# The split of the next expert weights is put before the copies of the combine weights on ScalarE and VectorE

## The reference

```python
scores = softmax(x @ gate_w.T)                  # 16 experts
topk_w, topk_ids = top_k(scores, 6)
combine = einsum('tk,tke->te', topk_w, one_hot(topk_ids, 16))
for e in range(16):                             # inner width 176
    out += combine[:, e, None] * (silu(x @ g_e.T) * (x @ u_e.T)) @ w2_e.T
out += (silu(x @ sg.T) * (x @ su.T)) @ sw2.T    # shared expert, inner width 352
```

## Time and profile before

| what | value |
|---|---|
| median of 3 launches | 911.11 us (910.43 to 911.59) |
| the profiled launch, its own time | 910.82 us |
| its span in the trace | 909.0 us |
| PE busy | 887.6 us (98%) |
| DVE, ACT, POOL busy | 615.3 us, 424.0 us, 101.3 us |
| experts of layer 0 and layer 1 | about 93 to 300 us and 700 to 906 us of the span |

### The profile page before, as it was taken

One profiled execution on the slowest core, in us unless ns is written; L12 is line 12 of the kernel. 1 busy time (PEld: TensorE's weight loads), 2 busy tenths in 40 slices (PEclk: granted clock), 3 DMA queues, 4 the chain that ended last, 5 costly groups with the idle time before them and its releaser, 6 DMA issues.

```text
span 909.0 us, 14200 instructions
## 1 busy us (share of the span) xinstructions
PE 887.6 (98%) x5377; PEld 687.1 (76%) x5377; DVE 615.3 (68%) x1185; ACT 424.0 (47%) x1063; POOL 101.3 (11%) x128
## 2 busy tenths in 40 slices
PE   8998999999999999999999999999999999999998
PEld 5665778888888876667877777777767778888886
DVE  4679656666666667657787786877785566666665
ACT  8554643343443479863543444344354444333342
POOL 4011000000000220003122232322210000000000
PEclk9999999999999999999999999999999999999999
DMA  6003111111100500006200000000010111111001
GB/s 189 1 7 119 36 52 53 39 48 52 35 0 1 231 1 2 1 1 265 91 2 1 1 1 1 1 1 2 0 36 18 36 53 52 53 35 52 17 0 47
DMA packets 12537, 37.10 MB, mean 41 GB/s; under 512 B 2080, under 2 KB 4352, under 8 KB 11712
## 3 DMA queue, kind: packets, MB, share of 16 engines
q1 hardware_dynamic: 12448, 36.32, 12.0%
q0 software_dynamic: 32, 0.01, 0.0%
HBM read 35.27 MB, written 1.05 MB: 40 GB/s over the span
## 4 chain that ended last, share of the span: by engine, by line
PE 85%; DVE 7%; ACT 5%; DMA 1%; issue 1%; POOL 0%; DVEq 0%; ACTq 0%
PE ps L1345 79%; PE ps L1978 3%; PE ps L1518 2%; DMA wx<-in_wx 1%; DVE P L542 1%; ACT Q L1134 1%; DVE stats L466 1%; ACT DT L950 1%; DVE xn L474 0%; ACT probs_q L1252 0%; ACT whi L1149 0%; DVE weighted_h L694 0%; DVE probs_q L866 0%; PE ps L1356 0%; DVE wlo L810 0%
## 5 line engine op out<-in xcount | busy, mean ns | idle before, releaser
L1179 ACT ACTIVATE h_hi<-weighted_h 128x512 fp32r<-128x512 f32 x100 | 63.2, 632 | 150.9 <-DVE weighted_h L694 148.8
L704 DVE TENSOR_TENSOR h_lo<-weighted_h,h_hi 128x512 fp32r<-128x512 f32 x100 | 69.2, 692 | 66.1 <-ACT h_hi L1179 65.9
L1345 PE MATMUL ps<-xT_first,whi 128*128 128x512 f32 x376 | 109.0, 391 | 1.2 <-ACT silu_g L1174 1.2
L1345 PE MATMUL ps<-xT_second,whi 128*128 128x512 f32 x376 | 108.5, 391 | 1.3 <-ACT silu_g L1174 1.2
L731 DVE TENSOR_TENSOR shared_gate<-silu_g,row_shares 128x512 f32<-128x512 f32 x88 | 60.9, 692 | 61.2 <-ACT silu_g L1174 61.0
L1174 ACT ACTIVATE silu_g<-ps 128x512 f32<-128x512 f32 x100 | 59.7, 598 | 73.4 <-PE ps L1345 73.4
L1345 PE MATMUL ps<-xT,merged_q 128*128 128x256 f32 x384 | 91.9, 383 | 0.0
L1337 POOL TENSOR_TENSOR latent_rot<-rope_buf 128x256 f32<-128x256 f32 x96 | 68.4, 733 | 180.4 <-DVE rope_buf L821 180.4
L1345 PEld LDWEIGHTS ps<-xT_first,whi 128*128 128x128 f32 x376 | 70.3, 188 | 17.3 <-issue 2.8
L1345 PEld LDWEIGHTS ps<-xT_second,whi 128*128 128x128 f32 x376 | 70.1, 188 | 17.0 <-issue 2.5
L1345 PEld LDWEIGHTS ps<-xT,merged_q 128*128 128x128 f32 x384 | 70.4, 190 | 10.5
(11 more groups left out here) (197 smaller groups left out, 1572.7 us busy)
## 6 DMA issues: line engine op xcount, KB each, us to landing
raw<-in_ffn SPq DMA_DIRECT2D x50, 384.0 KB, 3.0
wx<-in_wx SPq DMA_DIRECT2D x4, 2048.0 KB, 11.2
cx<-in_cx SPq DMA_DIRECT2D x1, 1536.0 KB, 8.2
X<-in_x SPq DMA_DIRECT2D x4, 256.0 KB, 6.8
kvc<-in_kvc SPq DMA_DIRECT2D x1, 1024.0 KB, 14.3
out<-X SPq DMA_DIRECT2D x4, 256.0 KB, 2.2
wqkv<-in_wqkv SPq DMA_DIRECT2D x1, 768.0 KB, 8.2
wqkv<-in_wqkv SPq DMA_DIRECT2D x1, 512.0 KB, 6.3
```

The costliest lines, as they stand in the source:

```text
L704: v.tensor_tensor(h_lo[:, u % 2, :], weighted_h[:, u % 2, :], h_hi[:, u % 2, :].bitcast(F32), ALU.subtract).then_inc(act_lo[l], 1)
L1179: a.activation(h_hi[:, u % 2, :], weighted_h[:, u % 2, :], ACT.Copy).then_inc(act_hi[l], 1)
L1345: return pe.matmul(o, l, r, start=start, stop=stop, skip_group_check=True)
```

## The change

In both programs the call that splits the next chunk moves ahead of the work on the combine weights. Nothing is added or removed, and PE's and SP's programs are untouched.

```diff
 # program of DVE
                         act_low(l, n, u)
                         if isinstance(n, int) and n == EARLY:
                             router_choice(l, 1)
-                        if isinstance(n, int) and n in (4, 6):
-                            combine_rest(l, n // 2 - 2)
                         ahead = next_split(i, last, u)
                         if ahead is not None:
                             split_lo(l, i * RING + ahead, ahead % RING)
+                        if isinstance(n, int) and n in (4, 6):
+                            combine_rest(l, n // 2 - 2)
 # program of ACT
                         act_high(l, n, u)
+                        ahead = next_split(i, last, u)
+                        if ahead is not None:
+                            split_hi(l, i * RING + ahead, ahead % RING, i + ahead // RING)
                         if isinstance(n, int) and n in (4, 6):
                             hf = n // 2 - 2
                             a.wait_ge(pe_combine_t, 2 * l + hf + 1)
...
                             a.wait_ge(pe_row_shares, 2 * l + hf + 1)
                             a.activation(row_shares[:, hf, :], ps[:, 7, :], ACT.Copy).then_inc(row_shares_copied, 1)
-                        ahead = next_split(i, last, u)
-                        if ahead is not None:
-                            split_hi(l, i * RING + ahead, ahead % RING, i + ahead // RING)
```

## The result

The changed kernel takes 908.15 us in the median of 10 launches (907.40 to 909.74), the kernel before 910.84 us in the median of 10 (910.43 to 911.59). The ratio is 0.9972, with a 95% interval from 0.9963 to 0.9982. In a second group of runs it was 0.9965 (0.9951 to 0.9979). The forecast was 908.2 us.

The account below looks back on a forecast made before the run. PE bounds the kernel, busy 887.6 of 909.0 us, so time is won only where it stands. Four places at 0.72 us, 2.88, say 2.9, off 911.11 give 908.2 us; own range 907.5 to 908.9, 8 in 10 907.2 to 909.4.

Parts of the forecast that it names:

- Where the kernel stood: PE ahead of the gate products of steps 6 and 8 in each layer: four waits for `silu_g`, 2.3 us in all.
- The loss at one place, 0.83 us: Gate product of step 6, layer 0: starts 0.75 us late, first two matmuls 0.08 us slower; four places 3.3 us at most.
- The gain at one place, 0.72 us: `silu_g` follows the copy into `shares` directly, so the gate product moves from 114.07 to 113.35; bounds 0.72 and 0.83 us.
- What stays, 0.11 us: Left of the stall at each gate product: 0.03 us of late start and 0.08 us of a late weight load.
- Moved work at no cost: Four `whi` copies fit ACT's idle time, tightest early by 0.74 us; four `wlo` subtractions fit DVE's, early by about 0.4 us.
- slower rival: A late `whi` copy holds `shares`, `silu_g` and PE, from a start after 122.31 in step 6; 913 us possible; chance 3%.
- VectorE: Subtractions for `wlo` ahead of `combine_rest` cost nothing; `h_lo` of step 5 or 7 then comes early enough for an early PE.
- The unbroken piece of PE: From step 7 on PE alone sets the pace, 155.84 and 164.26 us in the two layers; earlier gains arrive in full.
- a gain swallowed later: Rival: a reload or the hand-over to the next stage takes back a quarter or all; 908.9 to 911.1 us; chance 9%.
- a change without effect: Rival: something else holds the gate product as late as `silu_g`, PE still starts at 114.07; 911.1 us; chance 3%.
- All of the wait goes: Rival: the weight load is hidden too and `silu_g` comes slightly sooner; gain 3.3 us, 907.8 us; chance 6%.

Follow-up runs that it names:

- step 6 alone: Against the kernel before, both engines' order changed at step 6 only, step 4 left as it was: 909.49 us, ratio 0.9985.
- `silu` ahead: Against the changed kernel, `silu` of steps 5 and 7 also put ahead of the copy into `shares`: 907.61 us, ratio 0.9963; again 907.12 us, 0.9959.
- one more copy: Against the changed kernel, one unread copy of the raw chunk added ahead of the copy into `whi` at each of four places: 907.68 us, ratio 0.9965.
- two more copies: Against the changed kernel, two unread copies of the raw chunk added ahead of the copy into `whi` at each of four places: 909.59 us, ratio 0.9985.
- ScalarE's part alone: Against the changed kernel, VectorE's old order restored, `combine_rest` ahead of the subtraction for `wlo`; only ScalarE's order stays changed: 908.73 us, ratio 0.9974.
- VectorE's part alone: Against the kernel before, only VectorE's order changed, the subtraction for `wlo` ahead of `combine_rest`; ScalarE as before: 911.75 us, ratio 1.0011.

## Why the prediction was right

- **Where the kernel stood.** The four waits of PE for `silu_g` were the place. They are gone from PE's waits, and with step 6 alone exactly two of them, 1.2 us, stay.
- **The loss at one place, 0.83 us.** From the first transpose of step 4 to the second pair of the gate product it was 114.61 - 111.49 = 3.12 us, in the changed kernel 113.83 - 111.45 = 2.38 us, with `silu` ahead 114.05 - 111.76 = 2.29 us. So all that could be had is 0.83 us, as worked out.
- **The gain at one place, 0.72 us.** Measured 3.12 - 2.38 = 0.74 us at step 4 of layer 0. At all four places the weight load of the gate product comes 0.72 to 0.74 us sooner behind `h_hi`. `silu_g` behind the copy into `shares` started as forecast but lasted 0.57 us, not the 0.59 us taken from the pair at `row_shares`. 4 x 0.74 is 2.96 us against the 2.88 us forecast; the medians of the first group differ by 2.7 us, the spans by 3.1 us.
- **What stays, 0.11 us.** Measured 0.09 us; by the steps between matmuls above it is 0.02 us of a later start and 0.06 us of a slower first pair. The run with `silu` ahead shows that both come from a `silu_g` that ends only as PE gets there.
- **Moved work at no cost.** Right on both engines, and the runs give its limits: one more copy fits, the second does not. The second one is the mechanism of the slower rival, but not that outcome: that rival began where `whi` starts only after the transposes have released the copy into `shares`, the point from which the kernel is slower than before. With two more copies `whi` starts at 122.63 us in step 6 of layer 0, some 0.2 us ahead of that release, and the kernel is still faster than before. A part of the gain is lost already from a start 0.74 us ahead of the release, because that is how long the copy into `shares` queues behind it.
- **VectorE.** The prediction costed its part at nothing and said that behind `combine_rest` the next product comes early enough. What it left without a price is what this is worth: ScalarE's part alone gets a new wait of which 0.38 and 0.37 us reach the ends of the two layers.
- **The unbroken piece of PE.** The argument was right, but a length was misread. The 155.84 us of the earlier trace rows end at 280.09 us, where the view that was asked for ended, and not where the piece ends; so the length that the prediction said should stay could not be read. Up to the end of layer 0's experts the views show it whole, before and then after:

```profile
124.25 162.88 PE ps L1345 x715
...
121.50 164.13 PE ps L1345 x721
```

It ends at 287.13 and at 285.63 us. The piece of after starts earlier only because no wait breaks it at the gate product of step 8; from that product on (122.74 us) it is 162.89 us. Behind it the last steps of the layer run over DVE and ACT in turn, before and after, and these move up by the same 1.5 us.

- **Nothing is given back.** 1.50 us are there at the first transfer behind layer 0 and 1.67 us at the start of layer 1's experts; layer 1 adds 1.48 us up to the output. The two rivals of a gain swallowed later and of a change without effect fall.
- **All of the wait goes.** This rival was not what the change did; it took one more move to get there.

## What to carry to other kernels

- When an engine stands ahead of a copy that waits for another engine, look at what is queued behind the copy: independent work belongs ahead of the wait, and work that the bound engine wants next belongs ahead of independent work.
- An order is moved on all engines that share the step, or the wait returns one engine further: here half of the move won 2.1 us, the other half alone lost 0.9 us, and together they won 2.7 us (by medians of two groups; the traces put the worth of the second half beside the first at 0.75 us).
- Cover can be counted from the rows, idle time before the waiting instruction against the start-to-start distance of what is put there, and a run with a dummy copy checks it.

## What the runs showed of the hardware

- All profiled launches do not start alike. The instructions up to `h_hi` of step 4 in layer 0 are the same in all versions, yet it starts at 108.49 to 109.96 us. In the launch at 109.96 us PE waits 0.81 us at 14.74 us for a copy of `qk`, in that of the kernel before 0.30 us at 14.44. So the distances within a trace are a better measure than the spans; what makes the difference was not looked for.
- Between the experts of the two layers 0.17 us more was won than layer 0 gave (1.67 against 1.50 us). The chain of the kernel before runs over a load of `wx` of 11.86 us there and that of the changed kernel does not. From the issue of `wx` to the start of layer 1's experts it is 389.09 us before and 389.04 us with VectorE's part alone, but 388.82 to 388.94 us in the profiled launches of all the other versions. So it recurs; its cause stays open.
